# A vision tower on one core: the norms' small steps go to VectorE, and the pipeline is laid out afresh

## The chip, the cores and the metric

One core of a Trainium2 chip runs the whole program. The metric is the device time of one execution in microseconds (us); the kernel before takes 4496.96 us (median of 3 runs, 4495.98 to 4497.75).

## The reference

64 images of 3x224x224 go through a patch embedding and two blocks; after each of the four halves `h = layernorm(h + part(h))`, without gain or bias, over 256 channels.

```
h = patches(x) @ W.T + b                       # 196 tokens of 256 channels
h = ln(h + mamba(h))    # in_proj to 512, conv of 4 taps, silu, x_proj to 33,
                        # softplus, scan over 196 tokens for 512 channels x 16 states,
                        # sum over states, layernorm over 512 ("y"), gate, out_proj
h = ln(h + sigmoid(r) * (relu(k)**2 @ Wv.T))   # token mix with the token before
h = ln(h + gamma * attention(h) + h)           # 8 heads, leaky-relu scores, softmax
h = ln(h + moe(h))                             # 8 experts, top 2
```

Everything is float32. So an image has five layernorms, called y, out, ffn, att and moe in the code.

## The kernel before

Each image is a list of stages, each with a slot number (`AT_...`, lines 61 to 150). A block of the program has 16 slots; every engine walks through blocks and slots, and in each slot does the stages whose number falls there modulo 16, for the image that this number belongs to. An image takes slots -46 to 84, so about eight images are in work at once, and in the steady part each block finishes one. The slots only set each engine's own order: within a slot the order is that of the engine's `step` function (SP line 434, GpSimd 511, TensorE 752, ScalarE 1008, VectorE 1275). What waits for what is set by semaphores alone.

The spine is the scan, 16 groups of 4 states per image. GpSimd multiplies `u` by the broadcast B rows into a ring of four X tiles (`inputs`, line 486), ScalarE makes the decays dA in PSUM, in a ring of two (`decay`, 915), VectorE scans (`scan_group`, 1145), GpSimd multiplies by the C rows (`times_c`, 497), and TensorE adds up the states (`sum_states`, 608). `drain_y` (922) copies a quarter of the sum out of PSUM; the quarter that ends with group 15 is its last.

The other stages lie between. Those that the prediction follows, by engine:

- TensorE: `patches` (563, in three parts), `embed` (575), `turn_y` (619), `turn_back` of out (636) and of ffn (636, from `rs`), `turn_probs` (689), `expert_pair` (738, four pairs); `keep_busy` (554), six matmuls whose result nobody needs, stands ahead of the scan's sums of slot 12.
- ScalarE: `softplus` (903), `drain_patches` (854), `tanh_of_z` (879), `probs` (987), `normalise` of y, ffn and att (947), `drain_pT` (998).
- VectorE: `moments` (1150, 1154: mean and variance of a norm), `add_tokens` (1263), `scale_pair` (1256, four per image, into a ring of two), `normalise` of out and moe (1159).
- SP issues every DMA: the image (`load`, 403, sixteen transfers of 64-byte pieces), the rows of B, C and dt (420), the experts' gates (`store_gates`, `spread_gates`, 426 and 432), the result (407).

The norms. VectorE takes the moments; GpSimd then does all of `inverse_std` (line 499): it adds epsilon (502), for y, ffn and att negates the mean (504), raises to the power -0.5 (506), and for those three multiplies the negated mean by it (509, "shift"). ScalarE then scales and shifts in one pass; VectorE, for out and moe, uses the mean and the power as they are.

Start: SP issues all 32 loads of weights, then the first image; ScalarE, VectorE and TensorE wait for all the weights (`w_landed`) before anything.

Of the kernel before, what the change touches and what calls it, by code (L numbers as in the profile page):

```python
# [18 lines left out]
BLK = 2  # L19
TB = T // BLK  # L20
D = 256
# [32 lines left out]
GIN = 3  # L54
LN_EPS = 1e-5
# [7 lines left out]
AT_LOAD = -46  # L63
AT_PATCH = (-30, -28, -26,)
AT_PATCH_OUT = (-29, -28, -26,)
AT_EMBED = -25
AT_EMBED_OUT = -24
AT_XB = -23
# [5 lines left out]
AT_XPROJ = -15  # L74
AT_XPROJ_OUT = -14
AT_PROJ_STORE = -27
AT_DT_LOAD = -21
AT_SOFT = -13
AT_U = -14
AT_IN = -3  # L80
# [3 lines left out]
AT_B = (-19, -19, -18, -18,)  # L84
AT_C = (-16, -17, -7, -13,)
AT_Y_OUT = (6, 11, 13, 19,)
# [3 lines left out]
AT_Y_STD = 19  # L90
# [4 lines left out]
AT_OUT = 26  # L95
# [6 lines left out]
AT_H1T_OUT = 31  # L102
AT_MIX = 31
AT_RK = 32
AT_RK_OUT = 33
# [5 lines left out]
AT_FFN_STD = 39  # L111
AT_FFN_NORM = 43
# [4 lines left out]
AT_VALUES = 47  # L117
AT_VALUES_OUT = 49
AT_SCORES = (45, 46, 47, 50,)
AT_TURN_P = (49, 51, 54, 56,)  # L120
AT_AV = (51, 53, 56, 58,)
AT_PR = (44, 45, 47, 51,)
AT_MAX = (46, 47, 48, 52,)
AT_PROBS = (46, 48, 53, 55,)
AT_PT = (50, 51, 53, 56,)
AT_AV_OUT = (53, 59,)
AT_TURN_AV = (54, 61,)
AT_MEET = (55, 60,)
AT_ATT = 60
AT_ATT_STD = 59  # L130
AT_ATT_NORM = 61
AT_H3T = 66
# [3 lines left out]
AT_GATE_EXP = 69  # L136
AT_TOP2 = 70
AT_WS = 71
AT_WS_OUT = 71
AT_GATE_STORE = 59  # L140
AT_GATE_LOAD = 59
AT_H3T2 = 75
AT_SCALE = (75, 76, 77, 78,)
AT_PAIR = (79, 79, 79, 80,)
AT_ACC_OUT = 80
AT_MOE_T = 82
AT_MOE_STATS = 82
AT_MOE_STD = 82
# [55 lines left out]
def vit_tower(nc, x, w_tok, b_tok, w_in, conv_w, conv_b, w_xproj, a_log, d_par, dt_w, dt_b, w_out, ln_g, ln_b,  # L204
              w_r, w_k, w_v, mu_r, mu_k, w_qk, b_q, b_k, w_vv, b_v, gamma, w_g, b_g, w_e, b_e,
              ident, q_mask, k_mask, rank_of, proj, gates, out):
    with ExitStack() as ctx:
# [46 lines left out]
        epsc = sb("epsc", [TB, BLK])  # L254
        mhalf = sb("mhalf", [TB, BLK])
        mone = sb("mone", [TB, BLK])
# [61 lines left out]
        def bank(name, tile, uses):  # L318
# [6 lines left out]
        x_landed = sem("x_landed")  # L325
        w_landed = sem("w_landed")
        out_landed = sem("out_landed")
        const_ready = sem("const_ready")
# [42 lines left out]
        dve_past = sem("dve_past")  # L371
# [4 lines left out]
        loads = [(wtok, w_tok), (btok, b_tok), (win, w_in), (cw, conv_w), (cb, conv_b), (wxp, w_xproj),  # L376
# [3 lines left out]
                 (idn, ident), (qmask, q_mask), (kmask, k_mask), (rk, rank_of)]  # L380
        W_ALL = 16 * len(loads)
        CONSTS = 14
# [10 lines left out]
        def _(sp):  # L393
            def load(s):
# [39 lines left out]
            def step(b, par):  # L434
                for g in range(GROUPS):
# [3 lines left out]
                    for s, q in at(AT_DT_LOAD):  # L439
                        after(sp, dt_ready, s)  # L440
                        spread_rows(s, dtin[:].rearrange("p (o t) -> p o t", o=1), 0, 1, dtin_landed)
                    for ng in range(GC):
# [4 lines left out]
                    for s, q in at(AT_PROJ_STORE):  # L447
                        store_proj(s)
                    for s, q in at(AT_STORE):
                        store_out(s)  # L450
                    for s, q in at(AT_GATE_STORE):
                        store_gates(s)
                    for ng in range(GC):
                        n0 = NG * ng
                        for s, q in at(AT_B[ng]):
                            after(sp, xs_pool, WIDES * s - WC + ng // 2 + 1)
                            spread_rows(s, Bb[:, n0:n0 + NG, :], 1 + n0, NG, B_landed[ng])
                    for s, q in at(AT_GATE_LOAD):
                        spread_gates(s)
                    for s, q in at(AT_LOAD):  # L460
                        load(s)

            for dst, src in loads:
                sp.dma_start(dst[:], src).then_inc(w_landed, 16)
# [4 lines left out]
        def _(pool):  # L469
# [41 lines left out]
            def step(b, par):  # L511
                for g in range(GROUPS):
# [3 lines left out]
                    for k in range(WIDES):  # L516
                        for s, q in at(2 * k + AT_IN):
                            inputs(s, q, k)
                    for s, q in at(AT_MOE_STD):
                        inverse_std(s, "moe")  # L520
                    for s, q in at(AT_ATT_STD):
                        inverse_std(s, "att")
                    for k in range(WIDES):
                        for s, q in at(2 * k + AT_TIMES):
                            times_c(s, k)
                    for s, q in at(AT_OUT_STD):
# [3 lines left out]
                    for s, q in at(AT_FFN_STD):  # L530
                        inverse_std(s, "ffn")
                    for s, q in at(AT_U):
                        make_u(s, q)

            nc.gpsimd.memset(h1T[:, :, 0:1], 0.0).then_inc(zeros_ready, 1)
            nc.gpsimd.memset(epsc[:], LN_EPS).then_inc(zeros_ready, 1)
            nc.gpsimd.memset(mhalf[:], -0.5).then_inc(zeros_ready, 1)
            nc.gpsimd.memset(mone[:], -1.0).then_inc(zeros_ready, 1)
            pool.wait_ge(zeros_ready, 4)
# [3 lines left out]
        def _(pe):  # L543
# [44 lines left out]
            def xproj(s):  # L588
                pe.wait_ge(S.drained, S.count("xb", s))
# [162 lines left out]
            def step(b, par):  # L752
                for g in range(GROUPS):
                    def at(slot):
                        return live(b, par, g, slot)

                    for part in range(3):
                        for s, q in at(AT_PATCH[part]):
                            patches(s, part)
                    for s, q in at(AT_MOE_T):  # L760
                        turn_moe(s)
                    for s, q in at(AT_H1T):
                        pe.wait_ge(where["outT"].drained, where["outT"].count("outT", s))
                        turn(s, "h1T", h1)
                    for s, q in at(AT_FFN_T):
                        pe.wait_ge(where["v"].drained, where["v"].count("v", s))
                        turn_back(s, "ffnT", rs)
                    for s, q in at(AT_WARM[0]):
                        keep_busy(WARM[0])
                    for s, q in at(AT_WARM[4]):  # L770
                        keep_busy(WARM[4])
# [3 lines left out]
                    for i in range(BLK):  # L775
                        for s, q in at(AT_TURN_AV[i]):
                            turn_values(s, i)
                    for s, q in at(AT_WARM[1]):
                        keep_busy(WARM[1])
                    for s, q in at(AT_Z):  # L780
                        project_in(s, hT[q], "z", IC)
                    for s, q in at(AT_XPROJ):
                        xproj(s)
                    for s, q in at(AT_RK):
                        pe.wait_ge(mix_step, 4 * (s + 1))
                        channel_major(s, "r", wr, xr)
                        channel_major(s, "k", wk, xk)
                    for n in range(UNITS):
                        for s, q in at(AT_AV[n]):
                            mix_values(s, q, n)  # L790
                    for s, q in at(AT_GATE):
                        gate(s, q)
                    for s, q in at(AT_TURN_Y):
                        turn_y(s)
                    for s, q in at(AT_WS):
                        turn_gates(s)
# [3 lines left out]
                    for s, q in at(AT_QK):  # L800
                        queries_keys(s)
# [622 lines left out]
```

## Time and profile before

| | us |
|---|---|
| median of 3 runs | 4496.96 |
| span of the profiled execution, first to last instruction | 4498.6 |
| GpSimd (POOL) busy | 4031.8 |
| TensorE (PE) busy | 4150.4 |
| ScalarE (ACT) busy | 3836.7 |
| VectorE (DVE) busy | 3749.3 |

No time of the profiled execution beside its span is given; the span itself is 1.6 us above the median of the runs. The first 300 us fill the pipeline, the last 250 us empty it, and between them the same pattern repeats once per image.

### The profile page before, as it was taken

The numbers are of one execution on the slowest core, as the hardware profiler recorded it, in microseconds if no ns is written. First come the engines' busy times: TensorE is split into PE (matmuls) and PEld (weight loads), VectorE is DVE, ScalarE is ACT, GpSimd is POOL, SyncE is SP. The second block draws the span as 40 slices with busy tenths as digits, with TensorE's granted clock in tenths as the row PEclk, the third lists the DMA queues.
The fourth block names the chain that finished last, engine by engine and source line by source line (L and its number), as shares of the span: only waits on it lengthen the run. The fifth ranks groups of instructions, "written<-read, shape, count | busy, mean of one in ns | idle before, by whom it ended". The sixth has DMA issues, their size and how long they took to land.

```text
span 4498.6 us, 92573 instructions
## 1 busy us (share of the span) xinstructions
PE 4150.4 (92%) x32128; PEld 3625.2 (81%) x32128; DVE 3749.3 (83%) x7246; ACT 3836.7 (85%) x10114; POOL 4031.8 (90%) x2120
## 2 busy tenths in 40 slices
PE   4689999999999999999999999999999999999986
PEld 3678888888888888888888888888888888888775
DVE  2678889888888888888988988888888888898853
ACT  3688988988988998898898898898899889889852
POOL 3999999999999999999999999999999999999930
PEclk8799999999999999999999999999999999999987
DMA  4332332233233233233233223323323323323200
GB/s 100 71 71 65 75 82 75 67 82 78 69 78 80 70 77 87 67 76 82 69 73 82 75 67 82 78 70 77 80 69 76 89 66 76 82 68 74 70 19 29
DMA packets 730609, 328.75 MB, mean 73 GB/s; under 512 B 631542, under 2 KB 655392, under 8 KB 729888
## 3 DMA queue, kind: packets, MB, share of 16 engines
q1 hardware_dynamic: 730144, 322.83, 29.1%
q8 instruction: 258, 4.23, 0.4%
q14 instruction: 207, 1.70, 0.1%
HBM read 307.82 MB, written 14.90 MB: 72 GB/s over the span
## 4 chain that ended last, share of the span: by engine, by line
PE 65%; ACT 19%; DVE 5%; POOL 5%; issue 3%; DMA 1%; SPq 1%; DVEq 0%; POOLq 0%; ACTq 0%
PE G L738 15%; PE YB L608 13%; PE G L575 6%; ACT dA L915 5%; PE SB L679 4%; PE G L660 4%; PE SB L584 4%; PE G L628 4%; PE G L652 3%; POOL X L497 2%; ACT pr L987 2%; PE SB L689 2%; POOL X L486 2%; DVE xbs L1110 2%; PE G L636 2%
## 5 line engine op out<-in xcount | busy, mean ns | idle before, releaser
L1145 DVE TENSOR_TENSOR_SCAN X<-dA,X 128x392 f32<-128x392 f32 x2048 | 1870.5, 955 | 142.0 <-ACT dA L915 96.7
L497 POOL TENSOR_TENSOR X<-X,Cb 128x1568 f32<-128x1568 f32 x512 | 1802.8, 3521 | 129.7 <-DVE X L1145 127.2
L486 POOL TENSOR_TENSOR X<-u,Bb 128x1568 f32<-128x1568 f32 x512 | 1804.2, 3524 | 0.1
L915 ACT ACTIVATE dA<-dt,negA 128x195 f32<-128x195 f32 x4096 | 1510.5, 414 | 64.6 <-DVE X L1145 46.0
L608 PE MATMUL YB<-idn,X 128*98 128x128 f32 x8192 | 1086.3, 276 | 23.6 <-POOL X L497 23.6
L608 PEld LDWEIGHTS YB<-idn,X 128*98 128x98 f32 x8192 | 908.2, 129 | 155.8 <-issue 102.1
L738 PE MATMUL G<-hg,we 128*128 128x196 f32 x4096 | 711.2, 332 | 8.3 <-DVE hg L1256 6.1
L738 PEld LDWEIGHTS G<-hg,we 128*128 128x128 f32 x4096 | 684.8, 192 | 10.8 <-issue 7.5
L987 ACT ACTIVATE pr<-pr,nmx 98x196 f32<-98x196 f32 x1024 | 453.4, 446 | 9.1 <-DVE nmx L1192 9.1
L584 PE MATMUL SB<-hT,win 128*128 128x196 f32 x2048 | 368.2, 333 | 14.5 <-ACT pT L998 5.6
L584 PEld LDWEIGHTS SB<-hT,win 128*128 128x128 f32 x2048 | 335.5, 190 | 29.5 <-issue 21.3
L575 PE MATMUL G<-patT,wtok 128*128 128x196 f32 x1536 | 278.1, 339 | 43.6 <-ACT patT L854 43.6
L575 PEld LDWEIGHTS G<-patT,wtok 128*128 128x128 f32 x1536 | 260.7, 195 | 57.3 <-issue 57.3
L979 ACT ACTIVATE pr<-SB 98x784 f32<-98x784 f32 x256 | 208.4, 814 | 111.8 <-PE SB L679 111.8
L1110 DVE SCALAR_TENSOR_TENSOR xbs<-SB,cw,xbs 128x195 f32<-128x195 f32 (+2 forms) x768 | 263.1, 407 | 40.7 <-ACT xbs L872 40.7
L689 PE MATMUL SB<-idn,pr 98*98 98x98 f32 x2048 | 226.6, 254 | 63.7 <-ACT pr L987 63.1
L1256 DVE TENSOR_TENSOR hg<-G,Gb 128x784 f32<-128x784 f32 x256 | 244.9, 957 | 44.9 <-PE G L738 24.6
L689 PEld LDWEIGHTS SB<-idn,pr 98*98 98x98 f32 x2048 | 182.5, 129 | 111.6 <-ACT pr L987 80.7
L1192 DVE TENSOR_REDUCE nmx<-pr 98x4 f32<-98x784 f32 x256 | 245.3, 958 | 22.2 <-ACT pr L979 3.4
L998 ACT ACTIVATE pT<-SB 98x784 f32<-98x784 f32 x256 | 208.4, 814 | 48.5 <-PE SB L689 48.3
L679 PE MATMUL SB<-km,qm 32*98 32x392 f32 x1024 | 233.4, 532 | 2.1 <-ACT pr L979 1.8
L947 ACT ACTIVATE h<-att,shift_att,rstd_att 98x256 f32<-98x256 f32 x128 | 69.9, 593 | 184.9 <-POOL shift_att L509 184.9
(151 smaller groups left out, 6554.7 us busy)
## 6 DMA issues: line engine op xcount, KB each, us to landing
Bb<-proj_rows SPq DMA_DIRECT2D x256, 392.0 KB, 4.2
Cb<-proj_rows SPq DMA_DIRECT2D x256, 392.0 KB, 3.8
Gb<-gate_rows SPq DMA_DIRECT2D x64, 784.0 KB, 4.1
px<-in_x SPq DMA_DIRECT2D x1024, 36.8 KB
out<-ob SPq DMA_DIRECT2D x64, 196.0 KB
dtin<-proj_rows SPq DMA_DIRECT2D x64, 98.0 KB, 3.0
we<-in_w_e SPq DMA_DIRECT2D x1, 2048.0 KB
proj_rows<-pj SPq DMA_DIRECT2D x64, 25.3 KB
```

Source lines behind the costliest of these rows:

```text
L486: tt(X[(WIDES * s + w) % RING][:], u[q % 2][:, c:c + 1, :].broadcast_to([P, NW, T]), Bb[:, n0:n0 + NW, :], ALU.mult).then_inc(xs_pool, 1)
L497: tt(t[:], t[:], Cb[:, n0:n0 + NW, :], ALU.mult).then_inc(prod_ready, 1)
L575: last = mm(o[:, m * T:(m + 1) * T], lhsT=wtok[:, k, m * P:(m + 1) * P], rhs=patT[:, half * COLORS + c, :], start=(k == 0), stop=(k == KP ...
L584: last = mm(o[:, j // 2, (j % 2) * T:(j % 2 + 1) * T], lhsT=win[:, k, m * P:(m + 1) * P], rhs=src[:, k, :], start=(k == 0), stop=(k == DC ...
L608: last = mm(YB[0:TB, k * P:(k + 1) * P], lhsT=x[:, n0 + j, k * TB:(k + 1) * TB], rhs=idn[:], is_transpose=True, start=False, stop=(g % GC ...
L679: last = mm(o[0:TB, j, :], lhsT=qm[mine, n % 2, k * TB:(k + 1) * TB], rhs=km[mine, :, :].rearrange("p h t -> p (h t)"), start=True, stop=True)
L689: last = nc.tensor.transpose(o[0:TB, j // 2, at:at + TB], pr[(UNITS * s + n) % PRING][:, j, k * TB:(k + 1) * TB], idn[:TB, :TB])
L738: last = mm(o[:, m * T:(m + 1) * T], lhsT=we[:, k, at:at + P], rhs=hg[p % GRING][:, e, k, :], start=(p == 0 and e == 0 and k == 0 and m == 0),
L915: last = go(dA[i % DRING][:, j, 1:T], dt_[q % 2][:, c, 1:T], ACT.Exp, scale=negA[:, c, n:n + 1])
L987: last = go(pr[i % PRING][:, j, :], pr[i % PRING][:, j, :], ACT.Exp, bias=nmx[i % PRING][:, j:j + 1], accum_out=esum[q % 2][:, n // 2, h:h ...
L1110: last = v.scalar_tensor_tensor(out=xbs[:, c, k:], in0=S.tile[:, c // 2, at:at + T - k], scalar=cw[:, c, TAPS - 1 - k:TAPS - k], in1=xbs[: ...
L1145: v.tensor_tensor_scan(t, dA[i % DRING].rearrange("p n t -> p (n t)"), t, 0.0, ALU.mult, ALU.add).then_inc(scan_done, 1)
```

## The change

1. Adding epsilon moves into VectorE's `moments`, as a fifth counted step. GpSimd keeps only the power. The shift becomes a VectorE stage of its own, `shift_of`, with slots of its own (y 20, ffn 42, att 64).
2. Nearly all slots and the order inside every engine's `step` are new.
3. The first loads are split: six of them (`head`) are issued by ScalarE, SP issues the first image ahead of the other 26 weights, and the constants made from these are computed later, ahead of the first gate of image 0.

```diff
-AT_LOAD = -46
-AT_PATCH = (-30, -28, -26,)
-AT_PATCH_OUT = (-29, -28, -26,)
+AT_LOAD = -52
+AT_PATCH = (-30, -28, -27,)
+AT_PATCH_OUT = (-29, -28, -27,)
...
-AT_ATT = 60
-AT_ATT_STD = 59
-AT_ATT_NORM = 61
+AT_ATT = 61
+AT_ATT_STD = 61
+AT_ATT_SHIFT = 64
+AT_ATT_NORM = 64
...
-AT_GATE_STORE = 59
-AT_GATE_LOAD = 59
+AT_GATE_STORE = 53
+AT_GATE_LOAD = 60
...
-AT_SCALE = (75, 76, 77, 78,)
-AT_PAIR = (79, 79, 79, 80,)
+AT_SCALE = (75, 77, 78, 78,)
+AT_PAIR = (79, 79, 80, 80,)
...
             def inverse_std(s, n):
-                pool.wait_ge(stats_step[n], 4 * (s + 1))
-                steps = 3 if n in shift else 2
-                tt(veps[n][:], mv[n][:, :, 1], epsc[:], ALU.add).then_inc(rstd_step[n], 1)
-                if n in shift:
-                    tt(shift[n][:], mv[n][:, :, 0], mone[:], ALU.mult).then_inc(rstd_step[n], 1)
-                pool.wait_ge(rstd_step[n], steps * (s + 1) - 1)
+                pool.wait_ge(stats_step[n], NSTEPS * (s + 1))
                 tt(rstd[n][:], veps[n][:], mhalf[:], ALU.pow).then_inc(rstd_step[n], 1)
-                if n in shift:
-                    pool.wait_ge(rstd_step[n], steps * (s + 1))
-                    tt(shift[n][:], shift[n][:], rstd[n][:], ALU.mult).then_inc(shifted[n], 1)
...
             def moments(s, n, src):
...
+                dve.wait_ge(stats_step[n], NSTEPS * s + 2 * BLK)
+                v.tensor_scalar(veps[n][:], mv[n][:, :, 1], LN_EPS, None, ALU.add).then_inc(stats_step[n], 1)
+
+            def shift_of(s, n):
+                dve.wait_ge(rstd_step[n], s + 1)
+                v.scalar_tensor_tensor(out=shift[n][:], in0=mv[n][:, :, 0], scalar=-1.0, in1=rstd[n][:], op0=ALU.mult,
+                                       op1=ALU.mult).then_inc(shifted[n], 1)
```

What the new slots and orders do to the stages that the prediction speaks of: on ScalarE the third part of the patches is drained one slot earlier (slot 5, ahead of `probs` 2, y's `normalise` and `drain_pT` 2; before, behind them), and att's `normalise` goes from slot 13 to slot 0 of the next block. On VectorE slot 11 has `scale_pair` 0 ahead of `add_tokens` (before, behind it), `scale_pair` 1 goes behind scan group 13, ffn's shift stands between scan group 10 and the taps. On TensorE `keep_busy` and the transpose `h3T2` stand ahead of `turn_back` of out. On GpSimd `inputs` goes from the first to the last place of a slot, a slot earlier; the powers of y and moe stand earlier. On SP the image's load stands between storing the gates and spreading them; before, it stood behind both.

## Rows read from the trace of the kernel before

**Rows 1.** The page's first part: busy us, share of the span, instructions.
```profile
PE 4150.4 (92%) x32128; PEld 3625.2 (81%) x32128; DVE 3749.3 (83%) x7246; ACT 3836.7 (85%) x10114; POOL 4031.8 (90%) x2120
```
**Rows 2.** The chain that ended last, longest pieces: start us, us, what.
```profile
1974.04 7.99 PE G L738 x48
2040.59 7.99 PE G L738 x48
```
**Rows 3.** The chain that ended last, one image (2041 to 2108).
```profile
2064.74 1.02 PE YB L608 x8
...
2078.96 0.71 ACT pT L998
...
2080.96 0.46 ACT patT L854
...
2101.02 0.99 PE YB L554 x6
...
2106.79 0.34 PE G L644 x4
```
**Rows 4.** Timeline of PE: start us, us, what [idle before <-releaser].
```profile
2079.81 0.86 PE L619 MATMUL SB<-idn,ysb 98*128 98x98 f32 x8 [0.45 <-ACT pT L998]
...
2081.66 4.22 PE L575 MATMUL G<-patT,wtok 128*128 128x196 f32 x24 [0.60 <-ACT patT L854]
...
2100.40 0.62 PE L636 MATMUL G<-idn,hT 128*98 128x128 f32 x4 [0.30 <-DVE hT L1263]
```
**Rows 5.** Groups by line and shape: busy us, mean ns | idle before, releasers.
```profile
L486 POOL TENSOR_TENSOR X<-u,Bb 128x1568 f32<-128x1568 f32 x512 | 1804.2, 3524 | 0.1
...
L1154 DVE BATCH_NORM_AGGREGATE mv_att<-stat_att 98x2 f32<-98x6 f32 x128 | 16.0, 166 | 9.5 <-issue 0.2
...
L502 POOL TENSOR_TENSOR veps_att<-mv_att,epsc 98x2 f32<-98x2 f32 x64 | 12.5, 195 | 99.7 <-DVE mv_att L1154 99.6
```
**Rows 6.** Timeline of POOL around att's norm.
```profile
2042.19 0.20 POOL L502 TENSOR_TENSOR veps_att<-mv_att,epsc 98x2 f32<-98x2 f32 x1 [1.13 <-DVE mv_att L1154]
...
2042.61 0.69 POOL L506 TENSOR_TENSOR rstd_att<-veps_att,mhalf 98x2 f32<-98x2 f32 x1
2043.38 0.19 POOL L509 TENSOR_TENSOR shift_att<-shift_att,rstd_att 98x2 f32<-98x2 f32 x1
```
**Rows 7.** Waits of all engines: us in total, times, longest us.
```profile
ACT h L947 <- POOL shift_att L509: 184.9, 63, 6.5
```
**Rows 8.** Lines 1244 and 1338 of DVE: ns min/median/max, first and last start us.
```profile
L1244 DVE RECIPROCAL gs<-gs x64: 165/166/167, 349.1 to 4468.6; 98x2 f32<-98x2 f32 x64
...
L1338 DVE TENSOR_SCALAR wv<-wv x1: 417/417/417, 24.3 to 24.3; 128x512 f32<-128x512 f32 x1
```
**Rows 9.** Timeline of DVE where the experts' first pair is scaled.
```profile
2099.70 0.55 DVE L1263 TENSOR_TENSOR hT<-G,hT 128x392 f32<-128x392 f32 x1
2100.18 0.96 DVE L1256 TENSOR_TENSOR hg<-G,Gb 128x784 f32<-128x784 f32 x1
```
**Rows 10.** Timeline of the SP queue, and the landing times of tile Gb.
```profile
2083.40 0.29 SPq L426 DMA_DIRECT2D gate_rows<-wsT  x1
...
2114.90 10.11 SPq L403 DMA_DIRECT2D px<-in_x  x16
...
DMA to landing us min/median/max: 3.7/4.1/5.9
```
**Rows 11.** Timeline of the start, all engines.
```profile
17.12 24.12 SPq L403 DMA_DIRECT2D px<-in_x  x32
24.02 0.17 DVE L1338 TENSOR_SCALAR cw<-cw 128x16 f32<-128x16 f32 x1 [24.02 <-DMA rk<-in_rank]
...
30.81 2.20 PE L563 MATMUL G<-idn,px 84*128 84x84 f32 x14 [30.81 <-DMA px<-in_x]
...
59.07 13.89 SPq L403 DMA_DIRECT2D px<-in_x  x16
...
77.52 1.45 ACT L915 ACTIVATE dA<-dt,negA 128x195 f32<-128x195 f32 x4
```

More of the change, by code:

```diff
@@ L514, in at @@
                         return live(b, par, g, slot)
[L516 to L520, printed above, removed]
                     for s, q in at(AT_ATT_STD):
                         inverse_std(s, "att")
+                    for s, q in at(AT_FFN_STD):
+                        inverse_std(s, "ffn")
                     for k in range(WIDES):
@@ L525, in step @@
                             times_c(s, k)
+                    for s, q in at(AT_MOE_STD):
+                        inverse_std(s, "moe")
                     for s, q in at(AT_OUT_STD):
@@ L759, in step @@
                             patches(s, part)
[L760 to L771, printed above, removed]
+                    for s, q in at(AT_WARM[2]):
+                        keep_busy(WARM[2])
+                    for s, q in at(AT_Z):
+                        project_in(s, hT[q], "z", IC)
+                    for s, q in at(AT_WARM[1]):
+                        keep_busy(WARM[1])
                     for p in range(PAIRS):
@@ L787, in step @@
                         channel_major(s, "k", wk, xk)
+                    for s, q in at(AT_WARM[3]):
+                        keep_busy(WARM[3])
                     for n in range(UNITS):
@@ L790, in step @@
                             mix_values(s, q, n)
[L791 to L796, printed above, removed]
                     for s, q in at(AT_H3T):
@@ L1018, in step @@
                             drain_patches(s, part)
+                    for n in range(UNITS):
+                        for s, q in at(AT_PR[n]):
+                            drain_scores(s, n)
+                    for s, q in at(AT_GATE_EXP):
+                        act.wait_ge(gate_step, GSTEPS * s + GIN)
+                        o = where["gate"].tile[0:TB, 0:BLK * EXPERTS]
+                        go(o, o, ACT.Exp).then_inc(gate_exp, 1)
+                    for s, q in at(AT_TAP):
+                        first_tap(s)
+                    for c in range(IC):
+                        for s, q in at(AT_Y_OUT[c]):
+                            drain_y(s, c)
+                    for s, q in at(AT_Z_OUT):
+                        tanh_of_z(s)
+                    for n in range(UNITS):
+                        for s, q in at(AT_PROBS[n]):
+                            probs(s, q, n)
+                    for s, q in at(AT_SOFT):
+                        softplus(s, q)
+                    for s, q in at(AT_EMBED_OUT):
+                        drain_embed(s, q)
+                    for i in range(BLK):
+                        for s, q in at(AT_AV_OUT[i]):
+                            drain_values(s, i)
                     for s, q in at(AT_WS_OUT):
@@ L1278, in at @@
                         return live(b, par, g, slot)
+                    for s, q in at(AT_MOE_STATS):
+                        o = filled("moeT", s)
+                        moments(s, "moe", lambda k: o[0:TB, k * D:(k + 1) * D])
                     for n in range(UNITS):
@@ L1287, in step @@
                             scan_group(s, k)
-                    for s, q in at(AT_OUT_NORM):
-                        normalise(s, "out", lambda k: where["outT"].tile[0:TB, k * D:(k + 1) * D], h1, where["outT"].drained)
+                    for s, q in at(AT_FFN_SHIFT):
+                        shift_of(s, "ffn")
                     for t, which in AT_TAPS.items():
@@ L1292, in step @@
                             taps(s, which)
+                    for s, q in at(AT_OUT_NORM):
+                        normalise(s, "out", lambda k: where["outT"].tile[0:TB, k * D:(k + 1) * D], h1, where["outT"].drained)
+                    for s, q in at(AT_Z_OUT):
+                        gate_z(s)
                     for i in range(BLK):
@@ L1304, in step @@
                             scale_pair(s, p)
+                    for s, q in at(AT_FFN):
+                        ffn_sum(s)
+                    for s, q in at(AT_MOE_NORM):
+                        after(dve, out_landed, 16 * s)
+                        normalise(s, "moe", lambda k: where["moeT"].tile[0:TB, k * D:(k + 1) * D], ob, where["moeT"].drained)
+                    for s, q in at(AT_FFN_STATS):
+                        o = filled("ffnT", s)
+                        moments(s, "ffn", lambda k: o[0:TB, k * D:(k + 1) * D])
+                    for s, q in at(AT_OUT_ADD):
+                        add_tokens(s, q)
+                    for s, q in at(AT_Y_STATS):
+                        dve.wait_ge(y_drained, IC * (s + 1))
+                        moments(s, "y", lambda k: ysb[:, k, :])
                     for s, q in at(AT_GATE_X):
```

375 lines of the change are left out of this document (185 added, 190 removed).

## The prediction

> **What bounds the kernel now.** I read the page's first part first: POOL is busy 90% of the span and PE 92%, DVE and ACT 83% and 85% [rows 1]. Four engines so close mean that the end is set by waits between them, so the chain of waits comes next. In its list of longest pieces the same piece returns after 2040.59 - 1974.04 = 66.55 us [rows 2]: that is what one image costs, and 62 such passes are what a change of the steady part is multiplied by.
>
> Inside one pass the chain has two stretches [rows 3]. It leaves PE at the end of the last sum of an image's states, 2064.74 + 1.02 = 2065.76, and runs through ACT (`drain_y`, softplus, decays, probabilities, y's norm) until the third patch drain ends at 2080.96 + 0.46 = 2081.42; PE starts `embed` at 2081.66 [rows 4]. That stretch is 15.90 us. From there to the next last sum, 2065.76 + 66.55 = 2132.31, the chain is PE's own work, 50.65 us. PE's idle time confirms it: 0.45 us for the turned probabilities ahead of `turn_y`, 0.60 us for the patches ahead of `embed`, 0.30 us for DVE's `add_tokens` [rows 4].
>
> POOL is not in this loop. One of its large instructions takes 3.524 us, and the group of 512 has 0.1 us of idle time before it [rows 5]; but it also waits 99.7 us in all for att's moments, which an engine that sets the pace would not do. Nor is ACT's largest wait a bound: it stands 184.9 us for att's shift, 2.9 us in each of 63 images [rows 7], at a place where the chain is on PE.
>
> **The change, part by part.**
>
> *POOL sheds.* Att's norm occupies POOL from 2042.19 to 2043.57, 1.38 us, of which the power is 0.69 [rows 6]. So y, ffn and att shed 0.69 us each; out and moe, which have one step ahead of the power, shed over half of the 2042.61 - 2042.19 = 0.42 us of att's two, some 0.27 each. Together 2.6 us per image. On the loop this is worth nothing, since POOL is not in it. In the first passes, while the pipeline fills and the late stages aren't there yet, it can be worth up to 2.6 us in three passes; I take 3 us in all, between 0 and 8.
>
> *DVE gains eight instructions per image*, five additions of epsilon and three shifts, of two elements on 98 partitions. The trace has no such row. From below: the reciprocal of the same size takes 0.166 us [rows 8]; each addition also waits for the moments just written, 9.5 us over 64 images or 0.15 us at the step ahead of it [rows 5]. That makes 8 x 0.17 + 5 x 0.15 = 2.1 us per image, and DVE has 17% of 66.55, 11 us, free. From above: an instruction that can't run beside POOL's waits out what POOL has under way, at most 3.52 us more each. I take the low end, because the nearest row in size and place, the reciprocal from SBUF to SBUF, was never longer than 0.167 us although POOL works through nearly all of the span [rows 1, 8]. The high end is the first rival below.
>
> *Att's shift comes late on purpose.* ACT's 2.9 us go, since att's `normalise` moves behind three slots of other work. Next late is PE's last sum, for which ACT then waits just the same; value 0. If the cover is gone, at most 2.9 us per image return.
>
> *ACT's stretch.* The third patch drain now stands ahead of probabilities, y's norm and `drain_pT`. So `embed` is no longer late, but `turn_y` still waits for `drain_pT`, and this is now behind the patch drain. Before, `drain_pT` ended at 2078.96 + 0.71 = 2079.67; adding 0.46 gives 2080.13. `turn_y` starts 0.14 later, as before (2079.81), and from it to `embed` PE needs 2081.66 - 0.60 - 2079.81 = 1.25 us [rows 3, 4]. So `embed` starts 15.76 us after the last sum instead of 15.90: 0.14 us gained per image.
>
> *DVE ahead of out's transpose.* `scale_pair` 0 (0.96 us [rows 9]) now stands ahead of `add_tokens`, and ffn's addition and shift (0.17 + 0.15, and 0.17) earlier in the same run of DVE, so the hT that PE wants comes 1.45 us later. PE comes later too: `keep_busy`, 0.99 us, and half of the turns at L644, 0.34 us, that stood behind this point or in another slot now stand ahead of it [rows 3]: 1.33 us. The wait of 0.30 [rows 4] becomes 0.30 + 1.45 - 1.33 = 0.42: 0.12 us lost per image. `scale_pair` 1 now comes behind a group of the scan, so PE may wait for it, between 0 and the 0.42 us of the wait just ahead; I take 0.10, nearer the low end, because PE is busy for 7.99 us with 48 matmuls of three pairs there [rows 2] and asks for the second only after the first.
>
> *SP.* The image's load now stands between storing and spreading the gates. It issues for 10.11 us [rows 10]. Stored at 2083.40 as before, the gates would be asked for at 2083.69 + 10.11 = 2093.8 and land 4.1 us later, 2097.9, or at worst 5.9 later, 2099.7. `scale_pair` 0 wants them at 2099.70, in `add_tokens`' old place [rows 9]. The 2 us of margin hide it; without them each late microsecond is one of PE's. B, C and dt behind it in the queue wait for POOL or ACT anyway.
>
> *Start.* PE begins at 30.81, when the first image has landed; its 16 transfers are issued behind all weights, from 17.12 on at 24.12 / 32 = 0.75 us each [rows 11]. Before, the sixteenth was issued at 17.12 + 12.1 = 29.2 and the image was there 1.6 us later; issued first, it is there near 14.5, 16 us earlier. The 26 other weights follow at 17.12 / 32 = 0.53 us each until 26 and land by 26 + 24.02 - 17.12 = 33, about when image 0's first gate wants the constants; DVE now makes them there, some ten instructions of 0.17 to 0.42 us [rows 8, 11], 2 us by estimate. 14 us remain up to the first decay (77.52 before). The rows of B for image 0 now queue behind the third image's load, 13.89 us [rows 11], which can take back up to 9 us. So 14 us, between 5 and 16.
>
> **The sum.** Per image -0.14 + 0.12 + 0.10 = +0.08 us, times 62 is +5. Span 4498.6 - 14 - 3 + 5 = 4486.6; the span stands 1.6 us above the median, so 4485. The working of each pass is good to about 0.3 us, so this case reaches from 4466 to 4504.
>
> **The rivals.**
>
> *The new DVE instructions wait for POOL* (slower). Place: ffn's addition and shift, out's addition and att's, all in the run of DVE between ffn's transpose and the second pair, for which PE waits. For it: in every two-input DVE group of the trace one operand is in PSUM (SB, G or dA), and none reads two tiles of SBUF; the three shifts will be the first. And the scaling of wv from SBUF to SBUF, 512 elements in 0.417 us, goes at 0.81 ns per element against 1.22 ns where one operand is in PSUM (0.96 us for 784 [rows 8, 9]), so that form, which the five additions have, uses a path of its own; it ran only at the start, when POOL had nothing to do. Against it: the reciprocal. Price: POOL is busy 90% of the time with 3.52 us instructions, so a random instruction waits 0.9 x 3.52 / 2 = 1.6 us. Out's addition finds POOL waiting for it; three waits, 4.8 us, lie on the run, and some 1.6 come back because later arrivals meet POOL idle: 3.2 us per image, 4485 + 62 x 3.2 = 4683, from 4560 to 4850. It decides once the run loses over 0.3 us. The Trainium skill has this as a rule (SBUF — State Buffer, "Who interferes with whom"): a VectorE instruction with two SBUF inputs, or a tensor_scalar in its two-port mode, shares a port pair with GpSimd, and the second to issue blocks until the first has finished. By that rule all eight would block; no row of this trace has both sides of it.
>
> *The loop comes loose* (faster). If ACT, rid of 2.9 us of waiting, runs ahead of the last sum, and POOL's products come early enough, PE's waits of rows 4 go and the pass nears PE's own work. Against: ACT's stretch begins with PE's sum whatever came before. Of the 1.35 us in rows 4 some 1.1 gone: 4485 - 62 x (1.1 + 0.08) = 4412, from 4400 to 4465.
>
> *The gates land late* (slower). If the load issues for 13.89 us, as at the start [rows 11], instead of 10.11, the gates land at 2101.7 and `scale_pair` 0, `add_tokens` and PE wait; with what PE has over there, 0.7 us of it: 4485 + 62 x 0.7 = 4528. Against: the margin of 2 us.
>
> **How the numbers follow.** Forecast 0.37, waits for POOL 0.32, loop loose 0.24, gates late 0.07. About 9 us (0.2%) either way of 4496.96 can't be told from no change: 4488 to 4506. The forecast's case is faster 0.19, same 0.14, slower 0.04. With the rivals: faster 0.19 + 0.24 = 0.43, same 0.14, slower 0.04 + 0.32 + 0.07 = 0.43. The range leaves out the ends of the two large rivals: 4410 to 4760; the forecast's own is 4466 to 4504.
>
> **What would show it.** Right: the pass between two expert pairs 66.4 to 66.9 us; no idle of PE ahead of `embed`; about 0.5 us ahead of out's transpose, released by DVE; first matmul near 15 us; POOL busy 2.6 us less per image. Wrong: the new DVE lines at over 0.5 us mean, or gaps ahead of them that end with a POOL instruction (first rival); idle time of DVE that ends with Gb (the gates); a pass under 65.6 us (loop loose); a first decay no earlier than 72.

## The result and the profile after: slower, 5005.4 us

The changed kernel takes 5005.4 us (median of 4 runs, 5005.1 to 5006.0) against 4497.4 us for the kernel before in the same comparison: ratio 1.1128, interval 1.1112 to 1.1143. The profiled execution's span is 5004.1 us. The forecast was 4485, the range ended at 4760, and even the slower rival's 4683 is far below.

The page's first part, and the chain's shares by engine, of the changed kernel; the first answers to [rows 1]:

```profile
PE 4291.0 (86%) x32128; PEld 3751.7 (75%) x32128; DVE 4442.9 (89%) x7758; ACT 3904.1 (78%) x10114; POOL 3909.9 (78%) x1414
...
DVE 57%; PE 15%; issue 14%; ACT 11%; POOL 2%; SPq 0%; DMA 0%; DVEq 0%; ACTq 0%; POOLq 0%
```

The chain's shares in the kernel before:

```profile
PE 65%; ACT 19%; DVE 5%; POOL 5%; issue 3%; DMA 1%; SPq 1%; DVEq 0%; POOLq 0%; ACTq 0%
```

DVE has 512 instructions more (8 for each of 64 images) and 693.6 us more of busy time: 1.35 us each, where 0.17 had been reckoned. POOL has 121.9 us less, 1.9 us per image. In the chain that ended last DVE now holds 57%, where it held 5%. In the chain's pieces, PE's `embed` returns after 1477.68 - 1402.78 = 74.90 us; [rows 2] had 66.55. The difference, 8.35 us, times 62 is 518 us: the loss is in the steady pass.

```profile
1395.27 2.05 DVE shift_y L1190
...
1402.78 5.81 PE G L576 x24
...
1470.17 2.06 DVE shift_y L1190
...
1477.68 5.81 PE G L576 x24
```

`shift_y`, two elements on 98 partitions, stands in this chain with 2 us. The groups by line and shape of DVE (busy us, mean ns | idle time before them) show the eight new ones:

```profile
L1190 DVE SCALAR_TENSOR_TENSOR shift_y<-mv_y,rstd_y 98x2 f32<-98x2 f32 x64 | 130.5, 2038 | 0.0
L1185 DVE TENSOR_SCALAR veps_ffn<-mv_ffn 98x2 f32<-98x2 f32 x64 | 128.4, 2007 | 2.2
L1190 DVE SCALAR_TENSOR_TENSOR shift_ffn<-mv_ffn,rstd_ffn 98x2 f32<-98x2 f32 x64 | 127.1, 1986 | 1.6 <-POOL rstd_ffn L512 1.6
L1185 DVE TENSOR_SCALAR veps_moe<-mv_moe 98x2 f32<-98x2 f32 x64 | 125.0, 1952 | 2.2
L1185 DVE TENSOR_SCALAR veps_att<-mv_att 98x2 f32<-98x2 f32 x64 | 109.9, 1718 | 2.2
L1190 DVE SCALAR_TENSOR_TENSOR shift_att<-mv_att,rstd_att 98x2 f32<-98x2 f32 x64 | 83.1, 1299 | 10.0 <-DVE accT L1307 9.7
L1185 DVE TENSOR_SCALAR veps_y<-mv_y 98x2 f32<-98x2 f32 x64 | 14.6, 228 | 2.2
L1185 DVE TENSOR_SCALAR veps_out<-mv_out 98x2 f32<-98x2 f32 x64 | 10.8, 169 | 2.2
```

Six of them take 1.3 to 2.0 us, two about 0.2 us, for the same arithmetic. The idle time before them is next to nothing: the trace books the wait as the instruction's own duration. What they wait for is seen by laying the timelines of DVE and POOL beside each other (start us, us). DVE:

```profile
2070.48 2.04 DVE L1190 SCALAR_TENSOR_TENSOR shift_y<-mv_y,rstd_y 98x2 f32<-98x2 f32 x1
2086.46 1.86 DVE L1185 TENSOR_SCALAR veps_ffn<-mv_ffn 98x2 f32<-98x2 f32 x1
...
2104.45 0.17 DVE L1185 TENSOR_SCALAR veps_out<-mv_out 98x2 f32<-98x2 f32 x1
2111.88 1.78 DVE L1185 TENSOR_SCALAR veps_att<-mv_att 98x2 f32<-98x2 f32 x1
```

POOL:

```profile
2068.99 3.51 POOL L497 TENSOR_TENSOR X<-u,Bb 128x1568 f32<-128x1568 f32 x1
2074.35 3.50 POOL L508 TENSOR_TENSOR X<-X,Cb 128x1568 f32<-128x1568 f32 x1 [1.84 <-DVE X L1175]
...
2084.76 3.54 POOL L497 TENSOR_TENSOR X<-u,Bb 128x1568 f32<-128x1568 f32 x1
...
2104.70 0.69 POOL L512 TENSOR_TENSOR rstd_out<-veps_out,mhalf 98x2 f32<-98x2 f32 x1 [1.18 <-DVE veps_out L1185]
...
2110.11 3.52 POOL L508 TENSOR_TENSOR X<-X,Cb 128x1568 f32<-128x1568 f32 x1 [1.23 <-DVE X L1175]
```

`shift_y` ends at 2072.52, POOL's product at 2072.50; `veps_ffn` at 2088.32, POOL at 2088.30; `veps_att` at 2113.66, POOL at 2113.63. `veps_out` meets an idle POOL, which waits for just this step, and takes 0.17 us. `veps_y` (median 0.17 us) starts in the last 0.10 to 0.12 us of a POOL product in 59 of 64 images and itself ends after it, so a wait could hardly show there. In all, 367 of the 512 new instructions took over 0.5 us; each of them began while POOL was at work and ended 0.01 to 0.03 us after the end of a POOL instruction.

The engines' waits (us in total, times, longest) show what follows, first in the changed kernel, then in the one before:

```profile
POOL X L508 <- DVE X L1175: 760.8, 430, 4.8
ACT dA L926 <- DVE X L1175: 432.5, 383, 3.2
```

```profile
POOL X L497 <- DVE X L1145: 127.2, 247, 12.3
```

DVE's scan comes late, POOL and ACT wait for it, and the pass grows: POOL waits six times as long for scans as before. POOL's line at 2074.35 shows one such wait, 1.84 us, for the scan that stood behind `shift_y`.

### The profile page after: what moved, and what is told of

Same layout as the page of the kernel before. It is cut to its first block, busy times and chain, and to the rows that moved or that the text cites. A ratio compares the mean times of both kernels' runs of the same rounds, so it can differ in the third digit from the quotient of the medians.

```text
span 5004.1 us, 92003 instructions
## 1 busy us (share of the span) xinstructions
PE 4291.0 (86%) x32128; PEld 3751.7 (75%) x32128; DVE 4442.9 (89%) x7758; ACT 3904.1 (78%) x10114; POOL 3909.9 (78%) x1414
## 4 chain that ended last, share of the span: by engine, by line
DVE 57%; PE 15%; issue 14%; ACT 11%; POOL 2%; SPq 0%; DMA 0%; DVEq 0%; ACTq 0%; POOLq 0%
DVE X L1175 24%; PE G L576 7%; DVE nmx L1229 4%; DVE hg L1293 4%; ACT dA L926 3%; DVE shift_y L1190 3%; PE YB L612 2%; ACT xbs L875 2%; ACT h L958 2%; DVE shift_att L1190 2%; DVE xbs L1121 2%; DVE stat_y L1180 1%; ACT xD L901 1%; PE G L648 1%; DVE ob L1196 1%
## 5 line engine op out<-in xcount | busy, mean ns | idle before, releaser
L926 ACT ACTIVATE dA<-dt,negA 128x195 f32<-128x195 f32 x4096 | 1536.0, 418 | 477.6 <-DVE X L1175 432.5
L742 PE MATMUL G<-hg,we 128*128 128x196 f32 x4096 | 721.4, 335 | 28.1 <-DVE hg L1293 26.1
L576 PE MATMUL G<-patT,wtok 128*128 128x196 f32 x1536 | 361.0, 408 | 6.9 <-ACT patT L857 6.8
L576 PEld LDWEIGHTS G<-patT,wtok 128*128 128x128 f32 x1536 | 344.0, 244 | 14.9 <-issue 6.2
L648 PE MATMUL G<-idn,h 98*128 98x98 f32 x1024 | 142.0, 265 | 171.4 <-ACT avT L1017 165.3
L648 PEld LDWEIGHTS G<-idn,h 98*128 98x128 f32 x1024 | 113.7, 151 | 186.3 <-ACT h L958 182.8
```

The costliest lines, as they stand in the source:

```text
L576: last = mm(o[:, m * T:(m + 1) * T], lhsT=wtok[:, k, m * P:(m + 1) * P], rhs=patT[:, half * COLORS + c, :], start=(k == 0), stop=(k == KP ...
L742: last = mm(o[:, m * T:(m + 1) * T], lhsT=we[:, k, at:at + P], rhs=hg[p % GRING][:, e, k, :], start=(p == 0 and e == 0 and k == 0 and m == 0),
L926: last = go(dA[i % DRING][:, j, 1:T], dt_[q % 2][:, c, 1:T], ACT.Exp, scale=negA[:, c, n:n + 1])
```

## Experiments

Theory P: the new instructions, in the forms that they have, can't run beside POOL's and wait for them. Rival L: the new layout, that is, slots and orders, is what is slow. Rival N: eight more instructions with their waits are too much for DVE, whatever their duration. The kernel before ran beside each group of four and took 4499.5, 4498.6 and 4498.1 us; differences below are to that.

**1. The steps back on GpSimd, all else kept.**

```diff
-                v.tensor_scalar(veps[n][:], mv[n][:, :, 1], LN_EPS, None, ALU.add).then_inc(stats_step[n], 1)
...
-                        shift_of(s, "ffn")
...
+                tt(veps[n][:], mv[n][:, :, 1], epsc[:], ALU.add).then_inc(rstd_step[n], 1)
+                if n in shift:
+                    tt(shift[n][:], mv[n][:, :, 0], mone[:], ALU.mult).then_inc(rstd_step[n], 1)
...
```

> The changed kernel with all small steps of the norms put back on GpSimd; its slots, orders and split loads stay. Theory P (each of the eight new two-element VectorE instructions waits until GpSimd's running instruction has ended, and VectorE with its 11 us per image became the bound): the pass falls from 74.90 us to about 66.5, VectorE's busy time from 4443 us to about 3720, the time to 5005 - 62 x 8.35 = 4487 us, from 4460 to 4500. Rival L (the new slots and orders are what is slow): the time stays within 30 us of 5005. Rival N (the sheer number of VectorE instructions and semaphore waits): 4487 too; the next run tells it from P.

4481.7 us, -17.8, ratio 0.9958 (0.9943 to 0.9973). L is out: slots, orders and loads are together a little faster. By its median it is also the fastest version of all those tried.

**2. The same steps on VectorE, each as two instructions of one element.**

```diff
-                v.tensor_scalar(veps[n][:], mv[n][:, :, 1], LN_EPS, None, ALU.add).then_inc(stats_step[n], 1)
+                for k in range(BLK):
+                    v.tensor_scalar(veps[n][:, k:k + 1], mv[n][:, k, 1:2], LN_EPS, None,
+                                    ALU.add).then_inc(stats_step[n], 1)
...
-                v.scalar_tensor_tensor(out=shift[n][:], in0=mv[n][:, :, 0], scalar=-1.0, in1=rstd[n][:], op0=ALU.mult,
-                                       op1=ALU.mult).then_inc(shifted[n], 1)
+                for k in range(BLK):
+                    v.tensor_scalar(shift[n][:, k:k + 1], mv[n][:, k, 0:1], rstd[n][:, k:k + 1], -1.0, ALU.mult,
+                                    ALU.mult).then_inc(shifted[n], 1)
```

> The changed kernel with each of the eight two-element steps on VectorE made into two tensor_scalar instructions of one element per partition (the shift with the power as a pointer scalar, so that only one tile is read as a tensor): 16 instructions in place of 8, the same arithmetic. Theory P, if it is the form that waits for GpSimd: about 0.17 us each, 16 x 0.17 = 2.7 us per image on VectorE in place of 11.4, VectorE busy near 3900 us, the time from 4460 to 4510. If the one-element forms wait as well: 16 waits, over 5005. Rival N (number of instructions): above 5005, near 5300. Rival L (layout): within 30 us of 5005 with short instructions.

4500.6 us (+1.0; ratio 1.0001, 0.9991 to 1.0011). Minimum, median and maximum in ns of two of the eight:

```profile
L1186 DVE TENSOR_SCALAR veps_ffn<-mv_ffn x128: 143/150/156, 214.7 to 4396.7; 98x1 f32<-98x1 f32 x128
L1193 DVE TENSOR_SCALAR shift_ffn<-mv_ffn,rstd_ffn x128: 185/202/213, 223.8 to 4397.8; 98x1 f32<-98x1 f32 x128
```

Not one of the 1024 waits (the longest takes 0.22 us), and 706 of them began and ended while POOL was inside an instruction. So 504.8 of the 508 us hang on the form, and N is out: twice the instructions, none of the loss. Against run 1, the move in short forms still costs 18.8 us, 0.3 us per image; the relief of POOL doesn't pay for it.

**3. The old layout with the steps on VectorE, two-element forms.** The stages `shift_of` stand behind the scan of slots 20, 42 and 61; slots, orders and loads are the old ones.

```diff
+AT_Y_SHIFT = 20
+AT_FFN_SHIFT = 42
+AT_ATT_SHIFT = 61
```

> The kernel before with nothing but the steps moved to VectorE (two-element forms; shift stages behind the scan of slots 20, 42 and 61); the old slots, orders and loads. Theory P: the eight groups have means of 1.3 to 2.0 us with GpSimd busy beside them, VectorE is at 11 us more per image, and the time is from 4750 to 5050. Rival L: within 30 us of 4497. Rival N as P, but with the eight at 0.17 us each and the time lost in waits.

5021.1 us, +521.5: P again. Only some groups are stretched here (medians 3.43 us for `veps_ffn`, 1.81 for `shift_ffn`, 1.47 for `veps_y`, 0.99 for `veps_moe`); the others meet an idle POOL. Run 5 shows that a part of the 521 has another cause.

**4. The old layout with the loads split, nothing else** (the diff's `head` and `load_rest`, and the constants ahead of the first gate).

```diff
+            for dst, src in head:
+                act.dma_start(dst[:], src).then_inc(head_landed, 16)
```

> The kernel before with nothing but the first loads split (six by ScalarE, the first image ahead of the other 26; constants ahead of image 0's first gate). The prediction's step gave 14 us up to the first decay, and the trace of the changed kernel shows 77.52 - 66.30 = 11.2: 4497 - 11 = 4486 us if the start counts in full (4480 to 4490). If the pipeline's filling hides the start, 4497. In either case the pass stays 66.55 us.

4486.4 us, -13.2, ratio 0.9968 (0.9955 to 0.9981, which is 8.5 to 20 us); the pass stays 66.55 us, and the start counts in full.

**5. Run 3 with the one-element forms.**

> The kernel before with the steps moved to VectorE in the one-element forms (16 instructions per image), old slots, orders and loads. Theory P: all short, 0.15 us for an addition and 0.2 us for a shift as in the changed kernel with these forms; the 524 us that the two-element forms cost in this layout are gone: 4497 plus the 19 us that 16 short instructions cost in the new layout (4500.6 against 4481.7), 4500 to 4525. If the place of the steps in the old order is what hurts and not the form: over 4700.

4658.3 us, +159.7: a miss. The forms account for 5021.1 - 4658.3 = 363 us, not for 524. All 16 are short (medians of 149 and 202 to 209 ns), but one stage waits:

```profile
DVE shift_y L1153 <- POOL rstd_y L502: 125.2, 63, 3.0
```

**6. Run 5 with GpSimd's power of y one slot earlier**, where the changed kernel has it.

```diff
-AT_Y_STD = 19
+AT_Y_STD = 18
```

> The kernel before with the steps on VectorE in the one-element forms (4658 us), and GpSimd's power of y one slot earlier (18 for 19, as in the changed kernel), ahead of the large instruction of slot 19. In that run VectorE stood 2.0 us per image at y's shift for the power, which GpSimd reached only behind 3.5 us of other work, and GpSimd then stood 3.7 us for the scan. Theory Q (that wait in VectorE's order is what the old layout charges): the 2.0 us go, 4658 - 62 x 2.0 = 4534 us, from 4500 to 4560. Rival: the 16 short instructions themselves don't fit the old orders: 4640 or more.

4519.2 us, +21.1: that wait is no longer among the larger ones, and 139.1 us went with it (125 were expected). What is left is about run 2's 18.8 us against run 1. DVE takes its instructions in order, so at y's shift it stood until POOL had made the power, and in the old slot POOL came to the power only behind a 3.5-us product.

**7. Run 2 with that power put back to slot 19.**

> The changed kernel with the one-element forms (4500.6 us), and GpSimd's power of y put back to slot 19, where the kernel before has it. Theory Q: y's power comes one large instruction later, VectorE stands about 2 us per image at y's shift: 4500 + 62 x 2.0 = 4620 us, from 4560 to 4660. Rival (the new slots give VectorE room for it): 4500 to 4515.

4512.9 us: only 12.4 us more than run 2. DVE waits 62.8 us for the power, about 1 us per image, and most of it is absorbed. That misses the expected 4560 to 4660: the earlier slot is worth 139 us in the old layout and 12 in the new one, and why the new one absorbs it was not tried.

**8. Additions in one element, shifts as they are.**

> The changed kernel with the five additions in the one-element form and the three shifts as they are, scalar_tensor_tensor of two elements with two tiles of SBUF as inputs. Theory P: the shifts keep means of 1.3 to 2.0 us, the additions take 0.15 us; VectorE gets 5.3 + 1.5 = 6.8 us per image more than before in place of 11.4. If VectorE still sets the pace: 74.90 - 4.6 = 70.3 us per pass, 4720 us, from 4640 to 4790. If only what exceeds its 11 us of slack counts: 4500 to 4520.

4699.2 us, +200.6. The additions take 149 ns, the shifts keep means of 1.94, 2.02 and 1.36 us. So the shifts wait without the additions beside them (run 12 shows an addition by itself), and free time on DVE doesn't absorb three such waits.

**9. As run 8, each shift as two `scalar_tensor_tensor` of one element.**

```diff
-                v.scalar_tensor_tensor(out=shift[n][:], in0=mv[n][:, :, 0], scalar=-1.0, in1=rstd[n][:], op0=ALU.mult,
-                                       op1=ALU.mult).then_inc(shifted[n], 1)
+                for k in range(BLK):
+                    v.scalar_tensor_tensor(out=shift[n][:, k:k + 1], in0=mv[n][:, k, 0:1], scalar=-1.0,
+                                           in1=rstd[n][:, k:k + 1], op0=ALU.mult,
+                                           op1=ALU.mult).then_inc(shifted[n], 1)
```

> The changed kernel with the five additions in the one-element form and each shift as two scalar_tensor_tensor of one element, still with two tiles of SBUF as inputs. What decides about the wait: if it is reading two tensors from SBUF, whatever their size, the first of each pair is stretched to a mean of over 1 us and the time is as in the run with two-element shifts or above, 4640 to 4900; if an instruction of one element escapes in any form, all are near 0.2 us and the time is 4490 to 4510.

4823.7 us, +325.1, worse than run 8. Groups of the shifts:

```profile
L1193 DVE SCALAR_TENSOR_TENSOR shift_y<-mv_y,rstd_y 98x1 f32<-98x1 f32 x128 | 128.6, 1043 | 0.0
L1193 DVE SCALAR_TENSOR_TENSOR shift_ffn<-mv_ffn,rstd_ffn 98x1 f32<-98x1 f32 x128 | 232.2, 1853 | 1.6 <-POOL rstd_ffn L512 1.6
```

With two tiles of SBUF as inputs even one element waits: the first of the pair nearly always, and for ffn both in 29 of 64 pairs. So two different properties matter: for the addition the number of elements, for the shift the second tensor input; the pointer scalar of run 2 reads the same power and doesn't wait.

**10. The changed kernel with GpSimd's products in halves.**

```diff
...
+                for j in range(2):
+                    last = tt(t[:, j * h:(j + 1) * h, :], t[:, j * h:(j + 1) * h, :],
+                              Cb[:, n0 + j * h:n0 + (j + 1) * h, :], ALU.mult)
+                last.then_inc(prod_ready, 1)
```

> The changed kernel, two-element forms kept, but each of GpSimd's 32 large instructions per image split into two of half the elements. Theory P: a stretched VectorE instruction ends with GpSimd's shorter instruction, so the six stretched groups fall from means of 1.3 to 2.0 us to 0.7 to 1.0 us, none of them near 3.5 us, and VectorE's busy time by some 5 us per image. GpSimd pays for twice the instructions (1.85 us for a half-size one against 3.52 us for a whole one: 0.18 us each, 5.8 us per image). The time between 4650 and 4900, with GpSimd about as busy as VectorE. If the wait has another cause than the running instruction, the means stay.

4936.2 us, just above the expected bound of 4900, and the shifts went the wrong way: `veps_ffn` 0.58 and `veps_moe` 0.52 us, but `shift_ffn` 4.78 us in the mean. One of these, DVE and then POOL (x2: two halves in one row):

```profile
2068.51 6.07 DVE L1198 SCALAR_TENSOR_TENSOR shift_ffn<-mv_ffn,rstd_ffn 98x2 f32<-98x2 f32 x1
```

```profile
2067.28 3.69 POOL L514 TENSOR_TENSOR X<-X,Cb 128x784 f32<-128x784 f32 x2
2070.88 3.68 POOL L499 TENSOR_TENSOR X<-u,Bb 128x784 f32<-128x784 f32 x2
2079.02 1.84 POOL L514 TENSOR_TENSOR X<-X,Cb 128x784 f32<-128x784 f32 x1 [4.46 <-DVE X L1183]
```

It stands over four POOL instructions in a row and ends, at 2074.58, where POOL itself must stop (2074.56), to wait 4.46 us for the scan behind the very instruction that it held up.

**11. Halves with a wait of GpSimd between them.**

```diff
...
+                    if j:
+                        pool.wait_ge(half_c, WIDES * s + w + 1)
...
```

> The changed kernel (two-element forms), GpSimd's large instructions in halves as in the run before, and now GpSimd waits between the halves for the first one's result. In the run without that wait a shift of ffn stood for 6.04 us, over four halves in a row, and came through only where GpSimd itself had to wait. Theory B (a waiting VectorE instruction gets in only where GpSimd pauses, not at every end of an instruction): with the pause none stands longer than one half, 1.9 us; shift_ffn's mean falls from 4.8 us to about 1; VectorE's busy time falls by some 5 us per image; 4650 to 4850 us. If a wait of GpSimd on its own result is no such pause: as before, 4936 us and shift_ffn at 4.8 us.

4595.4 us, +97.4, 341 us less than run 10 and below the expected 4650. Two of the groups (ns, minimum, median, maximum):

```profile
L1203 DVE TENSOR_SCALAR veps_moe<-mv_moe x64: 168/1844/1870, 398.3 to 4588.6; 98x2 f32<-98x2 f32 x64
...
L1208 DVE SCALAR_TENSOR_TENSOR shift_ffn<-mv_ffn,rstd_ffn x64: 143/687/697, 229.3 to 4492.4; 98x2 f32<-98x2 f32 x64
```

`shift_ffn` never exceeds 0.70 us; `veps_moe` stands for one half, 1.84 us. With pauses in POOL's stream a waiting instruction gets in at the next one. A single `shift_y` stood longer, 3.59 us, over two POOL instructions with no pause between them, and it too came in at the first pause.

**12. The old kernel with one two-element addition per image more**, behind the scan of slot 8, on a scratch tile that nobody reads.

```diff
+                            if k == 8:
+                                after(dve, dum_step, s)
+                                v.tensor_scalar(dum[:], mhalf[:], 1.0, None, ALU.add).then_inc(dum_step, 1)
```

> The kernel before with one more VectorE instruction per image and nothing else: a two-element tensor_scalar from SBUF to SBUF, on a scratch tile that nobody reads, behind the scan of slot 8. It prices one such wait where VectorE is not on the chain and has 11 us free per image. Theory F (time on VectorE within its free 11 us costs nothing, as the prediction reckoned for instructions off the chain): 4497 to 4505. Theory C (a stall of VectorE's scan is passed on by the rings to GpSimd and ScalarE): mean near 1.6 us, and up to 62 x 1.6 = 100 us more, 4520 to 4600.

4556.5 us, +58.5. One of them on DVE's timeline, and POOL's product beside it:

```profile
2049.88 1.16 DVE L1292 TENSOR_SCALAR dum<-mhalf 98x2 f32<-98x2 f32 x1
```

```profile
2047.51 3.51 POOL L488 TENSOR_TENSOR X<-u,Bb 128x1568 f32<-128x1568 f32 x1
```

It ends at 2051.04, POOL at 2051.02. DVE's busy time rises by 69.9 us, 1.1 us per image, and 58.5 us of that come out as time, in a kernel whose DVE is 83% busy and not in the loop's chain. What carries it out of DVE are again waits for the scan, ACT's above all; first before, then in this run:

```profile
POOL X L497 <- DVE X L1145: 127.2, 247, 12.3
ACT dA L915 <- DVE X L1145: 46.0, 90, 3.0
```

```profile
POOL X L499 <- DVE X L1147: 157.5, 308, 12.7
ACT dA L917 <- DVE X L1147: 107.9, 90, 3.4
```

Theory C, that the rings pass a stall of the scan on to GpSimd and ScalarE, holds. This addition reads its two elements side by side, where those of the norms read every second one, so the wait doesn't hang on that.

Taken together: VectorE's busy time beyond run 2's (for run 3 beyond run 5's, for run 12 beyond that of the kernel before), and the device time that came with it.

| kernel | DVE busy more, us | time more, us | share |
|---|---|---|---|
| run 3, old layout | 395.5 | 362.8 | 92% |
| changed kernel | 572.9 | 504.8 | 88% |
| run 10, halves | 528.2 | 435.6 | 82% |
| run 9, one-element shifts, two inputs | 377.2 | 323.1 | 86% |
| run 8, only shifts | 264.9 | 198.6 | 75% |
| run 11, halves and pauses | 161.2 | 94.8 | 59% |
| run 12, one more addition | 69.9 | 58.5 | 84% |

In runs 10 and 11 POOL was also busy 140 and 181 us longer than in run 2, since it had twice the products, so their time isn't that of the stalls alone. Run 9's profile is that of its fastest execution, 4808.1 us, which would make the share 81%.

## Why the prediction was wrong

**The step that failed** is "DVE gains eight instructions per image": the low end of its two bounds was taken, 0.17 us each, because the reciprocal of [rows 8] was near in size and place and never waited. Measured were 1.35 us each, in DVE's busy time. The reciprocal doesn't wait in the changed kernel either, although 60 of its 64 ran wholly inside a POOL product:

```profile
L1281 DVE RECIPROCAL gs<-gs x64: 166/166/167, 350.2 to 4975.0; 98x2 f32<-98x2 f32 x64
```

It was near in size, operands and place, but it is another operation. What decides is the operation together with what it reads: the addition of run 12, two elements from SBUF to SBUF too, waits, and with one element (run 2) it doesn't. The row near in form was the other one of [rows 8], the scaling of wv: a multi-element tensor_scalar from SBUF to SBUF, which the prediction named and set aside; that row had no busy POOL beside it, so it could not rule a wait out. "The trace has no such row" is not so for the additions. Among the constants of the start it has a tensor_scalar of two elements from SBUF to SBUF, 155 ns, ahead of POOL's first product like the others, so it could not rule a wait out either:

```profile
L1343 DVE TENSOR_SCALAR omr<-mur 128x2 f32<-128x2 f32 x1 | 0.2, 155 | 0.0
```

For the shift there was no row at all. The first rival had the mechanism right, and the sign that the prediction gave for it, new DVE lines of over 0.5 us in the mean, came for six of the eight. The upper bound was too low too: "at most 3.52 us more" is one whole instruction of POOL, and the changed kernel has one `shift_ffn` of 5.64 us.

**The rival's price was too low as well.** Its duration was good: 1.6 us each, measured 1.3 to 2.0 for six of the eight, and out's addition found POOL waiting, as it said. What failed is that only three stalls "on the run" were counted, and part of them given back: 3.2 us per image, measured 8.35. The stalls off that run were given no price, as if DVE's free 11 us covered them. In the table 59 to 92% of the busy time that the stalls add comes out as device time: the scan stands behind the stalled instruction, POOL's second product and ACT's decay stand behind the scan in rings of four and two, and they don't catch up. A sign of that coupling stood in the trace before, and the prediction didn't use it: POOL's other group of 512, the products with C, waited 127.2 us for DVE's scan. In the passes from 1402 to 1477 and, in the kernel before, from 1974.04 to 2040.59 (window, us, busy us of PE, PEld, DVE, ACT and POOL, then granted clock, DMA share and GB/s):

```profile
1402.00:1477.00 75.00, 65.60 (x502) 57.48 (x502) 69.24 (x122) 60.96 (x158) 61.18 (x23) 0.98 0.27 67
```

```profile
1974.04:2040.59 66.55, 63.72 (x503) 55.81 (x503) 58.42 (x114) 59.79 (x159) 63.02 (x34) 1.00 0.32 76
```

DVE's busy time grows by 10.8 us and the pass by 8.35; DVE is idle 5.8 us even so. The granted clock, 0.98 and 1.00, is the upper level of 2.4 GHz for nearly all of both, and PE is busy only 1.9 us more, so the clock isn't what the pass lost.

The Trainium skill's rule (SBUF — State Buffer, "Who interferes with whom") says that a VectorE instruction with two SBUF inputs, or in its two-port mode, shares a port pair with GpSimd, and that whichever of the two issues second blocks until the first has finished. By that rule all eight would block where they meet a busy POOL, and the trace agrees: six do, out's addition finds POOL idle, and y's starts in the last 0.12 us of a product. On the length it differs: the rule ends the wait with the instruction that came first, while run 10 shows 6.07 us over four of them; there the measurement decides.

**The other steps**, with the failed one taken out by run 1: 4485 was forecast, and run 1, which has the new slots, orders and loads but leaves the steps on POOL, took 4481.7. That it is near is in part luck: run 1 has neither POOL's relief (-3) nor the 0.49 us of steps ahead of out's transpose. Without these the prediction's own terms give an estimate of 4462: PE's 0.30 us there would go in place of 0.12 lost, so -0.14 - 0.30 + 0.10 per image, -21 us in all.
- *Start*: 14 us forecast, 13.2 measured (run 4). PE's first matmul came at 15.78, the first decay at 66.30 where [rows 11] had 77.52, and POOL's products waited 9.4 us for B rows, nearly all of it ahead of the first, behind the third image's load:

```profile
15.78 2.19 PE L564 MATMUL G<-idn,px 84*128 84x84 f32 x14 [15.78 <-DMA px<-in_x]
```

- *Slots and orders*: +5 from the path, and by the same terms -21 with the steps on POOL; measured, run 1 against run 4, -4.6 us, which the spread of run 4's executions (4481.2 to 4491.0) doesn't tell from nothing. The small terms (patch drain, `add_tokens`, `scale_pair` 1) were not tried apart.
- *SP*: the margin held. The gates are asked for at 2087.84, behind a load that issued for 8.98 us where 10.11 was reckoned from [rows 10], and DVE waited for them three times in all.
- *POOL sheds*: 2.6 us per image forecast, 1.9 measured. What the relief is worth by itself no run shows; run 2 against run 1 puts the whole trade at a loss of 18.8 us.
- *Att's shift*: ACT's wait of 184.9 us [rows 7] fell to 83.3 and gained nothing that shows.

## What to carry to other kernels

Before moving a small step to VectorE beside a busy GpSimd, ask for its form, not only for its size: two tensors read from SBUF, or several elements from SBUF to SBUF in a tensor_scalar, paid 1.3 to 2.0 us here for 0.17 us of work, and the same step with one element and a pointer scalar paid nothing. Where no row of the trace has the form beside a busy GpSimd, the price is open up to the other engine's whole instruction and beyond (6.07 us in run 10), and the nearest row is the one with the same operation and the same operands. And a stall in an engine whose work feeds a short ring was not covered by that engine's idle share here: count all of them, not only those on the chain.

## What was not expected of the hardware

A wait for POOL can outlast POOL's running instruction. In run 3 one addition of two elements stood for 8.83 us, to 156.25:

```profile
147.42 8.83 DVE L1146 TENSOR_SCALAR veps_y<-mv_y 98x2 f32<-98x2 f32 x1
```

POOL's three instructions beside it ran without a pause, to 156.22:

```profile
147.41 3.53 POOL L498 TENSOR_TENSOR X<-X,Cb 128x1568 f32<-128x1568 f32 x1
150.87 1.87 POOL L476 TENSOR_TENSOR u<-dt,xbs 128x784 f32<-128x784 f32 x1
152.67 3.55 POOL L487 TENSOR_TENSOR X<-u,Bb 128x1568 f32<-128x1568 f32 x1
```

With whole products most waits ended at the first end; with halves those of `shift_ffn` lasted over four. The seven traces with such waits (the changed kernel, runs 3 and 8 to 12) have 1623 of them over 0.5 us, and each ended 0.01 to 0.04 us after the end of a POOL instruction. Where POOL then paused for over 0.05 us, the waiting instruction got in, 1060 times of 1060. Where POOL went on without a gap, it got in 563 times and was passed over 364 times; what decides there stays open. POOL itself lost nothing to it: its products took 3.51 to 3.52 us in the mean in the changed kernel, as before [rows 5].
